# Softmax applied after the value product: a change of staging in a fused cross-attention and FP4 feed-forward kernel

## The chip, the cores and the metric

The kernel runs on one core of a Trainium2 chip. The metric is the device time of one execution in microseconds, the median of several runs. TensorE is called PE below, VectorE DVE in the rows, ScalarE ACT, GpSimd POOL and SyncE SP.

## The reference

`x` is (2, 1024, 256), the context (2, 154, 256), with 16 heads of 64 columns.

```python
def xattn(query, key, value, ...):
    q = einsum("bnd,hdk->bhnk", query, proj_q) + bias_q      # k, v from the context in the same way
    logits = einsum("bhqk,bhnk->bhqn", q, k) / sqrt(64)
    heads = einsum("bhqn,bhnv->bhqv", softmax(logits), v)    # 154 keys
    return concat(heads) @ w_out.T
x = x + xattn(layernorm(x), ctx, ctx, ...)
x = x + ffn(layernorm(x), w_gate, w_up, w_down)              # FP4 block quantisation, silu(gate) * up, width 704
```

## The kernel before

**Precision.** Every matrix product but the transposes is made of three f16 products. A tile in f32 is split into a high half (a cast to f16, mostly by ScalarE) and a low half (f32 minus the high half, mostly by VectorE); `three` (L454) multiplies high by high, high by low and low by high.

**Stages.** A start (to some 31 us) loads and splits the weights, makes keys and the first queries. Then comes the loop over 64 *slots*: a slot n is one step i = n // 8 (of 8), one of two token tiles s = n // 4 % 2 of 128 rows, and one group of four heads, j = n % 4. In a step the batch is i // 4. After the loop follow 16 tiles of the FFN. Every engine has its own program, an order written out by hand, with semaphores between them.

**One slot.** PE computes the scores of four heads, 128 tokens by 4 x 154 keys (`score`, L591). VectorE takes the row maxima (`row_max`, L1036), ScalarE the exponentials with their row sums (`exps`, L805, the sums through `accum_out`), VectorE the reciprocals (`inverse`, L1042). POOL multiplies the exponentials by them (`norm`, L1297 and L1298) into `normal`, 5 chunks of 128 columns: one per head for the first 128 keys and a fifth in which the last 26 keys of the four heads lie 32 apart. The high half of `normal` is cast by ScalarE in odd slots (L816), by VectorE in even ones (L1049); the low half is made by VectorE where n % 8 is 2, 5 or 6 (L1055), by POOL in the other five of eight (L1304). SP issues one DMA transpose of both halves, 128 x 1280 f16 (`turn_p`, L435), into `pT`, keys as rows.

**Tasks.** Besides scores and projection, PE has *tasks*, each with one PSUM bank: `x` (transpose of normalised rows, L566), `q` (queries of two pairs of heads, L577, 12 matmuls of 256 columns), `v` (values, L508 to L527), `wo` (transposes of w_out, L501), `w` (FFN weights, L602, L607) and `h` (heads, L540 and L543: values as the stationary tile of 64 columns, `pT` as the moving one of 256 tokens, two heads side by side in the array, 12 such pairs; the result is heads transposed, as the projection needs it). `tasks_of(n)` lists those of a slot. The three banks 4, 5 and 7 are taken in turn (`task_bank`), and `next_task` (L492) makes PE wait until VectorE has made the low half of the task that had the bank before. ScalarE makes the high half of each task (`high`, behind its exponentials), VectorE the low half (`low`, behind the row maximum of the next slot):

```python
# PE                                   # VectorE, slot(n)
for n in range(SLOTS):                 row_max(n)                      # waits for score(n)
    score(n)                           if n >= 1: inverse(n - 1)
    if parts_of(n): project(*parts_of(n))   ...
    for t in tasks_of(n):              for t in tasks_of(n - 1): low(t)
        task(t)
```

A step before has 4 `q`, 4 `h` and 1 `x` task in its 8 slots, and in the first slots also 6 `v` (slots 0 to 5) and 4 `wo` (slots 6 to 9).

**Projection.** `project(i, p)` (L554 to L556), 6 matmuls of 256 columns per slot, adds into bank 6; `add_attention` (L1060) adds the sum to x and takes its statistics. In the slots run also, on VectorE, POOL and ScalarE, six pieces of the FFN weights' quantisation (block scales L1069 to L1073 in slot 1 of steps 1 to 6, L1131 and L1134 in slots 5 and 6, L1311, L1335, L855) and LayerNorm steps (slots 52 to 56).

Of the kernel before, what the change touches and what calls it, by code (L numbers as in the profile page):

```python
# [31 lines left out]
REST = L - P  # L32
RESTP = 32
SLOTS = 2 * STEPS * QUADS
CHUNK = 5 * P
# [64 lines left out]
def xattn_ffn_kernel(nc, x, ctx_in, proj_q, bias_q, proj_k, bias_k, proj_v, bias_v, w_out,  # L100
                     w_gate, w_up, w_down, out):
    with ExitStack() as ctx:
# [12 lines left out]
        v_h = sb("v_h", [P, B, H * DK], F16)  # L115
        v_l = sb("v_l", [P, B, H * DK], F16)
        vl_h = sb("vl_h", [P, B, QUADS, 4, DK], F16)
        vl_l = sb("vl_l", [P, B, QUADS, 4, DK], F16)
        pT = sb("pT", [P, 2, QUADS, 2, 5, 2 * P], F16)
# [10 lines left out]
        xnT_h = sb("xnT_h", [P, KC, B * P], F16)  # L130
        xnT_l = sb("xnT_l", [P, KC, B * P], F16)
        negmax = sb("negmax", [P, 2, H], F32)
        rsum = sb("rsum", [P, 2, H], F32)
        rinv = sb("rinv", [P, 2, H], F32)
# [7 lines left out]
        A2 = KC * W1 + 4 * D + F + FC * D + 2 * FP_ + 2 * FP_ + 2 * D  # L142
# [4 lines left out]
        def halves(part, n):  # L147
# [5 lines left out]
        cT_h, cT_l = (v.rearrange("p (c n) -> p c n", c=KC) for v in halves(a2[:, CT0:CT0 + KC * B * L], KC * B * L))  # L153
        ROWS0 = CT0 + KC * B * L
        ctx_rows = a2[0:L // 2, ROWS0:ROWS0 + 2 * B * D].rearrange("p (j d) -> p j d", j=2 * B)
        assert ROWS0 + 2 * B * D <= A2
        bv = pT[0:1, 1].rearrange("p j a c n -> p (j a c n)")[:, 0:4 * H * DK].bitcast(F32)
        bv_raw = bv[:, 0:H * DK]
        bv_h, bv_l = halves(bv[:, H * DK:2 * H * DK], H * DK)
        q_h, q_l = (raw["q"].bitcast(F16)[:, j * RAW:(j + 1) * RAW]  # L160
                    .rearrange("p (a t) -> p a t", a=PAIRS) for j in range(2))
        prob = arena[:, RAW:RAW + SC].rearrange("p (j n) -> p j n", j=QUADS)
        NORM0 = RAW + SC
        normal = arena[:, NORM0:NORM0 + QUADS * CHUNK].rearrange("p (j n) -> p j n", j=QUADS)
        XN0 = 4 * RAW - 4 * D
        assert NORM0 + QUADS * CHUNK <= XN0
# [3 lines left out]
        assert A2 - QUADS * CHUNK >= CT0 + KC * B * L  # L170
        hidT_h, hidT_l = (v.rearrange("p (a n) -> p a n", a=PAIRS) for v in halves(arena[:, 4 * RAW:5 * RAW], RAW))
# [23 lines left out]
        mark = [RAW]  # L195

        def over(n):
            mark[0] += n
            assert mark[0] <= XN0
            return arena[:, mark[0] - n:mark[0]]  # L200
# [29 lines left out]
        exp_done, rinv_ready, normed = sem("exp_done"), sem("rinv_ready"), sem("normed")  # L230
        high_act, high_dve = sem("high_act"), sem("high_dve")
        low_dve, low_pool = sem("low_dve"), sem("low_pool")
        turned = [sem("turned%d" % j) for j in range(QUADS)]
        proj_mm, proj_done = sem("proj_mm"), sem("proj_done")
        bv_scaled, bv_high, bv_low, ld_bv = sem("bv_scaled"), sem("bv_high"), sem("bv_low"), sem("ld_bv")
# [33 lines left out]
        def query_at(i, j):  # L269

            return 8 * (i - 1) + ((5, 6, 7, 8) if i == 1 else (4, 6, 8, 9))[j]

        def heads_at(i, j):

            return 8 * (i + 1) + (2, 3, 5, 7)[j]
# [5 lines left out]
        def tasks_of(n):  # L281

            out = [("x", i) for i in range(1, STEPS) if rows_at(i) == n]
            if n < len(VALUES): out.append(VALUES[n])
            elif n < len(VALUES) + len(WOUT): out.append(WOUT[n - len(VALUES)])
            out += [("h", i, j) for i in range(STEPS - 1) for j in range(QUADS) if heads_at(i, j) == n]
            out += [("q", i, j) for i in range(1, STEPS) for j in range(QUADS) if query_at(i, j) == n]
            out += [("w", k) for k in range(W1_JOBS) if wt_at(k) == n]
            return out

# [632 lines left out]
        def _(dve):  # L923
# [212 lines left out]
            def slot(n):  # L1136
# [3 lines left out]
                if n >= 1: inverse(n - 1)  # L1140
# [251 lines left out]
```

## Time and profile before

| | us |
|---|---|
| median of 3 runs | 429.55 (426.49 to 430.19) |
| the profiled execution | 429.8 |
| its span, first to last instruction | 427.9 |
| mean granted PE clock | 0.932 of 2.4 GHz |

The rows further down are of this one profiled execution. Times are microseconds from the start of its span; a duration marked mean is in ns. "Idle before" is time in which the engine sat idle ahead of an instruction, and the arrow names what ended it. Instructions on one engine overlap a little at their ends, so two of 0.47 us take 0.84.

### The profile page before, as it was taken

The page shows a single profiled execution, that of the slowest core. Times are in us where ns is not written, and L with a number is a line of the kernel's source. Part 1 is how long each engine was busy: PE and PEld are TensorE (multiplying, and loading weights), DVE is VectorE, ACT ScalarE, POOL GpSimd, SP SyncE. Part 2 cuts the span into 40 slices and gives each one's busy share as a digit, 9 for nine tenths or more (in the row PEclk, how much of TensorE's full clock was granted, in tenths as well). Part 3 has the DMA queues.
Part 4 walks back from the last instruction along what each step waited for, and adds up shares of the span by engine and source line. Part 5 has one row for each costly group of instructions (what it writes and reads, how often), then busy time and mean ns, then how long its engine had stood idle before and what let it go on. Part 6 is the DMA issues. An engine that isn't in the chain of part 4 may idle for free.

```text
span 427.9 us, 9077 instructions
## 1 busy us (share of the span) xinstructions
PE 337.4 (79%) x3371; PEld 250.3 (58%) x3371; DVE 363.5 (85%) x652; ACT 259.6 (61%) x821; POOL 273.2 (64%) x275
## 2 busy tenths in 40 slices
PE   1865877876969969869687698198877999999985
PEld 1542355665747757757465466076655766677764
DVE  2989558899999997999999969448999999999692
ACT  4756578877787877877884678334351545543331
POOL 3453455897888878978886568613592767686710
PEclk9999589998998979999999669689998999999999
DMA  7970343455554464655543434600000000000001
GB/s 218 323 282 1 63 92 63 82 105 96 93 102 86 93 117 86 109 84 91 106 85 73 93 63 92 123 2 2 2 0 15 12 26 12 21 19 12 27 25 38
DMA packets 92413, 32.44 MB, mean 76 GB/s; under 512 B 84492, under 2 KB 90320, under 8 KB 92369
## 3 DMA queue, kind: packets, MB, share of 16 engines
q1 hardware_dynamic: 92369, 31.86, 34.7%
q8 instruction: 27, 0.44, 0.4%
q14 instruction: 17, 0.14, 0.1%
HBM read 8.78 MB, written 2.10 MB: 25 GB/s over the span
## 4 chain that ended last, share of the span: by engine, by line
DVE 58%; PE 18%; POOL 14%; issue 5%; ACT 3%; DMA 1%; SPq 0%; DVEq 0%; POOLq 0%
DVE negmax L1036 6%; POOL arena L1304 5%; POOL arena L1298 5%; DVE arena L1049 5%; DVE arena L1055 4%; DVE arena L1112 4%; DVE arena L1114 4%; DVE arena L998 3%; PE ps L456 3%; PE ps L458 3%; PE ps L591 3%; PE ps L457 3%; DVE arena L1027 3%; DVE arena L1238 3%; DVE blk_h L1069 2%
## 5 line engine op out<-in xcount | busy, mean ns | idle before, releaser
L805 ACT ACTIVATE arena<-ps,negmax 128x154 f32<-128x154 f32 x256 | 96.5, 395 | 46.8 <-DVE negmax L1036 46.5
L1297 POOL TENSOR_TENSOR arena<-arena,rinv 128x104 f32<-128x104 f32 x64 | 30.1, 470 | 64.5 <-DVE rinv L1042 64.5
L1298 POOL TENSOR_TENSOR arena<-arena,rinv 128x512 f32<-128x512 f32 x64 | 70.5, 1102 | 0.0
L1036 DVE TENSOR_REDUCE negmax<-ps 128x4 f32<-128x616 f32 x64 | 50.2, 785 | 20.5 <-PE ps L591 20.3
L1304 POOL TENSOR_TENSOR arena<-arena 128x640 f16<-128x640 f32 x40 | 63.7, 1592 | 0.8 <-ACT arena L816 0.8
L591 PE MATMUL ps<-kT_h,arena 64*128 64x154 f16 x512 | 39.8, 241 | 28.6 <-DVE arena L1027 18.7
L805 ACT ACTIVATION_READ_ACCUMULATOR arena<-ps,negmax 128x1 f32 x256 | 53.8, 210 | 0.0
L591 PEld LDWEIGHTS ps<-kT_h,arena 64*128 64x128 f16 x512 | 24.0, 98 | 44.9 <-DVE arena L1027 27.0
L456 PE MATMUL ps<-arena,xnT_h 128*128 128x352 f16 x128 | 40.1, 313 | 3.2 <-DVE xnT_l L1122 3.2
L456 PE MATMUL ps<-xnT_h,wq_h 128*128 128x256 f16 x128 | 36.2, 283 | 7.9 <-DVE wot_l L984 2.5
L456 PE MATMUL ps<-arena 128*128 128x256 f16 (+2 forms) x120 | 36.1, 301 | 7.8 <-DVE arena L937 5.9
L457 PE MATMUL ps<-arena,xnT_h 128*128 128x352 f16 x128 | 40.0, 313 | 0.0
L458 PE MATMUL ps<-arena,xnT_l 128*128 128x352 f16 x128 | 40.0, 312 | 0.0
L540 PE MATMUL ps<-pT,v_h 128*64 128x256 f16 x256 | 35.7, 288 | 3.8 <-DVE wot_l L984 1.6
L554 PE MATMUL ps<-wot_h,arena 128*128 128x256 f16 x128 | 37.8, 295 | 1.0 <-DVE arena L998 0.3
L555 PE MATMUL ps<-wot_l,arena 128*128 128x256 f16 x128 | 37.5, 293 | 0.0
L556 PE MATMUL ps<-wot_h,arena 128*128 128x256 f16 x128 | 37.4, 292 | 0.0
L876 ACT ACTIVATE arena<-ps 128x704 f32<-128x704 f32 x16 | 12.1, 756 | 41.4 <-PE ps L458 41.4
L457 PE MATMUL ps<-xnT_l,wq_h 128*128 128x256 f16 x128 | 36.3, 283 | 0.0
L458 PE MATMUL ps<-xnT_h,wq_l 128*128 128x256 f16 x128 | 36.2, 283 | 0.0
L457 PE MATMUL ps<-arena 128*128 128x256 f16 (+2 forms) x120 | 36.0, 300 | 0.0
L458 PE MATMUL ps<-arena 128*128 128x256 f16 (+2 forms) x120 | 35.9, 299 | 0.0
(155 smaller groups left out, 1030.5 us busy)
## 6 DMA issues: line engine op xcount, KB each, us to landing
out_dram<-arena SPq DMA_DIRECT2D x16, 128.0 KB, 1.7
xs<-in_x_dram SPq DMA_DIRECT2D x2, 512.0 KB, 7.2
arena<-in_L_xattn_w_out_dram SPq DMA_DIRECT2D x1, 1024.0 KB, 11.8
pT<-arena SPq DMA_TRANSPOSE x64, 3.4
xs<-in_x_dram SPq DMA_DIRECT2D x2, 384.0 KB, 6.6
wffn<-in_L_ffn_w_down_dram SPq DMA_DIRECT2D x1, 704.0 KB, 9.5
wffn<-in_L_ffn_w_gate_dram SPq DMA_DIRECT2D x1, 640.0 KB, 7.8
wffn<-in_L_ffn_w_up_dram SPq DMA_DIRECT2D x1, 640.0 KB, 8.4
```

Source lines behind the costliest of these rows:

```text
L456: pe.matmul(o, a_h, b_h, start=start, stop=False)
L457: pe.matmul(o, a_h, b_l, start=False, stop=False)
L458: return pe.matmul(o, a_l, b_h, start=False, stop=stop)
L540: pe.matmul(o[u * DK:(u + 1) * DK, k * 256:(k + 1) * 256], vh[:, b, h * DK:(h + 1) * DK], pT[:, i % 2, j, part, 2 * k + u], start=n == 0, ...
L554: pe.matmul(o, a_h, wot_h[:, p], start=p == 0 and s == 0, stop=False, skip_group_check=True)
L555: pe.matmul(o, a_h, wot_l[:, p], start=False, stop=False, skip_group_check=True)
L556: last = pe.matmul(o, a_l, wot_h[:, p], start=False, stop=p == PAIRS - 1, skip_group_check=True)
L591: last = pe.matmul(ps[:, 2 * (j % 2) + u, k * L:(k + 1) * L], q[r, p, s * P:(s + 1) * P], kt[r, batch(i), p], start=n == 0, stop=n == 2)
L805: last = act.activation(prob[:, j, k * L:(k + 1) * L], ps[:, 2 * (j % 2) + k % 2, (k // 2) * L:(k // 2 + 1) * L], ACT.Exp, bias=negmax[:, ...
L1036: dve.tensor_reduce(negmax[:, s, 4 * j:4 * j + 4].rearrange("p (k u) -> p u k", k=2), v, AX.X, ALU.max, negate=True).then_inc(max_done, 1)
L1298: pool.tensor_tensor(main_of(normal, j), v[:, :, 0:P], r.to_broadcast([P, 4, P]), ALU.mult).then_inc(normed, 1)
L1304: pool.tensor_tensor(part_of(j, 1), normal[:, j], part_of(j, 0), ALU.subtract).then_inc(low_pool, 1)
```

## The change

- ScalarE's exponentials no longer give row sums and go unnormalised into `prob`, where the four heads now lie 160 columns apart: 640 columns, 5 full chunks of 128. They are split right there: the high half by ScalarE in every slot, the low half by VectorE where n % 4 is 1, else by POOL. POOL's `norm` is gone.
- The values are laid out to fit these chunks, in 8 parts, each with 64 columns, a column of ones and one of padding (`HB` = 66), zero where a chunk's row belongs to another head. Heads are one task per slot: `pT` is the stationary tile (128 keys by 128 tokens), the values are the moving one, of 66 or 132 columns, 5 chunks times 3 products. Tokens are now the rows of the result, and the ones give the row sum in column 64 of each head.
- VectorE takes the reciprocal of the sums and multiplies heads by it, 128x256 from PSUM to SBUF (`scale_hid`). ScalarE casts the high half, POOL subtracts the low half, and SP transposes both by DMA (128 x 512 f16, `turn_hid`); the projection reads the result.
- Heads of slot n are computed in slot n + 5, projected in slot n + 10 (after the slot's tasks rather than ahead of them). Queries of steps 2 to 7 are tasks of one pair, one per slot; their buffers, and those of the turned rows, are doubled. Values of batch 0 are tasks of slots 0 to 3, of batch 1 of slots 11 to 14 (each 16 matmuls of 256 columns); w_out is turned in slots 6, 8, 9 and 10.
- `task_bank` and `next_task` stay as they are.

```diff
+LP = 160
+CHUNK = 4 * LP
+CHUNKS = CHUNK // P
+RING_P = 2 * QUADS
+HB = DK + 2
+HEADS_LAG = 5
+PROJ_LAG = 10
+PARTS = [(c, a) for c in range(CHUNKS) for a in range(4) if c * P < (a + 1) * LP and (c + 1) * P > a * LP]
...
-        VALUES = [("v", b, n) for b in range(B) for n in range(3)]
+        VALUES = [("v", b, n) for b in range(B) for n in range(4)]
+        def values_at(b, n):
+            return n if b == 0 else 11 + n
+        def wot_at(n):
+            return (6, 8, 9, 10)[n]
         def rows_at(i):
-            return 8 * (i - 1) + (3 if i == 1 else 2)
+            return 3 if i == 1 else 8 * (i - 1) - 1
+        def query_at(i, p):
+            return 4 + p // 2 if i == 1 else 8 * (i - 1) + 1 + p
+        def pairs_of(i):
+            return 2 if i <= 1 else 1
...
+            out += [t for t in VALUES if values_at(t[1], t[2]) == n]
+            out += [t for t in WOUT if wot_at(t[1]) == n]
+            out += [t for i in range(1, STEPS) for t in query_tasks(i) if query_at(i, t[2]) == n]
+            out += [("h", n - HEADS_LAG)] if HEADS_LAG <= n else []
...
         def low_by_dve(n):
-            return n % 8 in (2, 5, 6)
+            return n % 4 == 1
...
+            def turn_hid(n):
+                i, s, j = place(n)
+                sp.wait_ge(hid_low, n + 1)
+                if n >= RING_P: sp.wait_ge(proj_mm, n - RING_P + 1)
+                sp.dma_start_transpose(hidT[:, j, :, :, s * P:(s + 1) * P].rearrange("p a k n -> p (a k) n"),
+                                       hsplit[:, j]).then_inc(hid_turned[j], 16)
             for n in range(SLOTS):
-                turn_p(n)
+                if n >= 1: turn_p(n - 1)
+                if n >= HEADS_LAG + 2: turn_hid(n - HEADS_LAG - 2)
...
+            def heads(n):
+                i, s, j = place(n)
+                b = batch(i)
+                pe.wait_ge(turned[j], 16 * (n // QUADS + 1))
...
+                o = next_task(("h", n))
+                order = range(CHUNKS)
+                parts = ((v_h, 0), (v_l, 0), (v_h, 1))
+                for k, (v, part) in enumerate(parts):
+                    for c in order:
+                        at = [m for m, (chunk, a) in enumerate(PARTS) if chunk == c]
+                        h0, h1 = PARTS[at[0]][1], PARTS[at[-1]][1] + 1
+                        last = pe.matmul(o[:, h0 * HB:h1 * HB], pT[:, s, j, part, c],
+                                         v[:, b, j, at[0]:at[-1] + 1].rearrange("p m k -> p (m k)"),
+                                         start=k == 0 and c == order[0], stop=k == 2 and c == order[-1], skip_group_check=True)
+                last.then_inc(task_mm, 1)
...
             for n in range(SLOTS):
                 score(n)
-                if parts_of(n): project(*parts_of(n))
                 for t in tasks_of(n):
                     task(t)
+                if n >= PROJ_LAG: project(n - PROJ_LAG)
...
                 i, m = divmod(n, 8)
-                if n >= 2 and high_by_act(n - 2): high_p(n - 2)
+                if n >= 1: high_p(n - 1)
+                if n >= HEADS_LAG + 2: high_hid(n - HEADS_LAG - 2)
                 exps(n)
...
+            def inverse(n):
+                dve.wait_ge(task_mm, TASK_AT[("h", n)] + 1)
+                dve.reciprocal(rinv[:, n % 2].unsqueeze(2), per_head(n)[:, :, DK:DK + 1]).then_inc(rinv_ready, 1)
+            def scale_hid(n):
+                dve.wait_ge(rinv_ready, n + 1)
+                wait(dve, hid_low, n - 1)
+                dve.tensor_tensor(hidden_f[:, n % 2].rearrange("p (r k) -> p r k", r=4), per_head(n)[:, :, 0:DK],
+                                  rinv[:, n % 2].unsqueeze(2).to_broadcast([P, 4, DK]), ALU.mult).then_inc(task_low, 1)
...
                 row_max(n)
-                if n >= 1: inverse(n - 1)
-                if n >= 2 and not high_by_act(n - 2): high_p(n - 2)
+                if n >= HEADS_LAG + 1: inverse(n - HEADS_LAG - 1)
                 if n >= 1:
                     for t in tasks_of(n - 1):
                         low(t)
-                if n >= 2 and low_by_dve(n - 2): low_p(n - 2)
+                if n >= 1 and low_by_dve(n - 1): low_p(n - 1)
...
-                if n >= 1: norm(n - 1)
-                if n >= 2 and not low_by_dve(n - 2): low_p(n - 2)
+                if n >= 1 and not low_by_dve(n - 1): low_p(n - 1)
+                if n >= HEADS_LAG + 2: low_hid(n - HEADS_LAG - 2)
```

Of the last slots' heads, those of slots 59 to 63 are tasks of the FFN's first three tiles (2, 2 and 1), and the projections of slots 56 to 63 follow there in pairs, in the first four tiles; each waits for its DMA transpose.

## Rows read from the trace of the kernel before

**Rows 1.** page, part 1: busy us (share of the span), instructions, by engine
```profile
PE 337.4 (79%) x3371; PEld 250.3 (58%) x3371; DVE 363.5 (85%) x652; ACT 259.6 (61%) x821; POOL 273.2 (64%) x275
```

**Rows 2.** windows, one loop step: PE, PEld, DVE, ACT, POOL busy; clock, DMA share, GB/s
```profile
165.70:193.40 27.70, 23.05 (x306) 18.39 (x304) 26.78 (x49) 22.11 (x85) 22.83 (x25) 1.00 0.58 96
```

**Rows 3.** costliest groups, 60 to 305 us: xcount | busy us, mean ns | idle before
```profile
L1298 POOL TENSOR_TENSOR arena<-arena,rinv 128x512 f32<-128x512 f32 x58 | 64.3, 1109 | 0.0
L1304 POOL TENSOR_TENSOR arena<-arena 128x640 f16<-128x640 f32 x37 | 59.5, 1607 | 0.8 <-ACT arena L816 0.8
L805 ACT ACTIVATION_READ_ACCUMULATOR arena<-ps,negmax 128x1 f32 x229 | 48.3, 211 | 0.0
...
L1049 DVE CAST arena<-arena 128x640 f16<-128x640 f32 x29 | 28.4, 979 | 1.8 <-POOL arena L1298 1.1
L1297 POOL TENSOR_TENSOR arena<-arena,rinv 128x104 f32<-128x104 f32 x58 | 27.5, 473 | 47.0 <-DVE rinv L1042 47.0
L1055 DVE TENSOR_TENSOR arena<-arena 128x640 f16<-128x640 f32 x23 | 26.8, 1165 | 0.0
...
L1027 DVE SCALAR_TENSOR_TENSOR arena<-ps,biasT,arena 128x256 f16<-128x256 f32 x56 | 23.8, 466 | 0.0
...
L816 ACT ACTIVATE arena<-arena 128x640 f16<-128x640 f32 x30 | 22.6, 754 | 4.6 <-POOL arena L1298 4.6
L998 DVE TENSOR_TENSOR arena<-ps,arena 128x512 f16<-128x512 f32 x32 | 21.7, 680 | 0.1
...
L765 ACT ACTIVATE arena<-ps 128x512 f16<-128x512 f32 x32 | 19.6, 616 | 4.6 <-PE ps L543 4.6
```

**Rows 4.** chain of waits, 57 to 70 us: start us, us, what
```profile
63.58 0.80 DVE negmax L1036
...
64.47 0.59 DVE wot_l L984
65.05 0.14 issue
65.19 0.27 PE ps L456
65.46 0.11 PE ps L457
...
66.66 0.53 PE ps L591 x12
```

**Rows 5.** timeline, VectorE, row maximum of slots 8, 16, 33, 34, 48, 63
```profile
67.21 0.80 DVE L1036 TENSOR_REDUCE negmax<-ps 128x4 f32<-128x616 f32 x1 [0.62 <-PE ps L591]
...
94.48 0.78 DVE L1036 TENSOR_REDUCE negmax<-ps 128x4 f32<-128x616 f32 x1
...
154.39 0.79 DVE L1036 TENSOR_REDUCE negmax<-ps 128x4 f32<-128x616 f32 x1
...
158.47 0.73 DVE L1036 TENSOR_REDUCE negmax<-ps 128x4 f32<-128x616 f32 x1
...
205.64 0.78 DVE L1036 TENSOR_REDUCE negmax<-ps 128x4 f32<-128x616 f32 x1
...
265.16 0.78 DVE L1036 TENSOR_REDUCE negmax<-ps 128x4 f32<-128x616 f32 x1
```

**Rows 6.** the transposes' line: duration ns of the issue; us to landing
```profile
L435 SPq DMA_TRANSPOSE pT<-arena x64: 1320/1339/2344, 43.1 to 274.6; - x64
...
DMA to landing us min/median/max: 3.3/3.4/5.1
```

**Rows 7.** timeline, PE, 137 to 152 us: two pairs of score matmuls
```profile
138.41 0.24 PE L591 MATMUL ps<-kT_h,arena 64*128 64x154 f16 x2
138.49 0.23 PE L591 MATMUL ps<-kT_l,arena 64*128 64x154 f16 x2
```

**Rows 8.** timeline, POOL, start: its first subtraction and the idle time before it
```profile
12.63 2.11 POOL L1283 TENSOR_TENSOR pT<-pT 1x1024 f16<-1x1024 f32 x1 [8.15 <-ACT pT L732]
```

**Rows 9.** timeline, PE, 264 to 303 us: first transpose of the FFN
```profile
275.69 0.69 PE L641 MATMUL ps<-ident,arena 128*128 128x128 f32 x2 [8.81 <-POOL arena L1319]
```

More of the change, by code:

```diff
@@ new lines, in fourth @@
+                def fourth(part, a):
+                    return part.rearrange("p (j r k) -> p r j k", r=4, k=DK)[:, a]
+                for u, (chunk, a) in enumerate(parts_of_values(n)):
+                    out_u = o[:, u * 256:(u + 1) * 256].rearrange("p (j k) -> p j k", k=DK)
+                    keys = slice(chunk * P % LP, chunk * P % LP + P)
+                    for c in range(KC):
+                        three(out_u, cT_h[:, c, b, keys], cT_l[:, c, b, keys], fourth(wv_h[:, c], a), fourth(wv_l[:, c], a),
+                              c == 0, False)
+                    pe.matmul(out_u, ones[:, :], fourth(bv_h, a), start=False, stop=False)
+                    last = pe.matmul(out_u, ones[:, :], fourth(bv_l, a), start=False, stop=True)
@@ L547, in project @@
[L547 to L553 removed]
+                pe.wait_ge(turned[j], 16 * (n // QUADS + 1))
+                if i % (STEPS // B) == 0 and s == 0 and j == 0:
+                    pe.wait_ge(task_low, TASK_AT[("v", b, 3)] + 1)
@@ new lines, in heads, with project @@
+                last.then_inc(task_mm, 1)
+            def project(n):
+                i, s, j = place(n)
+                pe.wait_ge(hid_turned[j], 16 * (n // QUADS + 1))
+                if n < QUADS: pe.wait_ge(task_low, TASK_AT[("wo", n)] + 1)
+                if s == 0 and j == 0: wait(pe, proj_done, i)
+                o = ps[:, PROJ_BANK, s * D:(s + 1) * D]
+                for k in range(2):
+                    p = 2 * j + k
+                    a_h, a_l = (hidT[:, j, part, k, s * P:(s + 1) * P] for part in range(2))
@@ L583, in score @@
                 if s == 0:
-                    pe.wait_ge(task_low, TASK_AT[("q", i, j)] + 1)
+                    pe.wait_ge(task_low, TASK_AT[("q", i, 2 * j + 2 - pairs_of(i))] + 1)
                 wait(pe, exp_done, m - 1)
+                q_h, q_l = (queries(i)[:, part] for part in range(2))
                 for k in range(2):
@@ L613, in task @@
                 if t[0] == "q": query(t[1], t[2])
[L614 removed]
+                if t[0] == "h": heads(t[1])
                 if t[0] == "w": turn_weights(t[1])
@@ L621, in task @@
                         pe.wait_ge(ones_ready, 1)
-                    values(t[1], t[2]) if t[2] < 2 else rest_values(t[1])
+                        pe.wait_ge(ctx_wide, 1)
+                    values(t[1], t[2])
             turn_x(0)
             pe.wait_ge(w_low, 2)
-            for j in range(QUADS):
-                query(0, j)
+            for t in query_tasks(0):
+                query(0, t[2])
             pe.wait_ge(job_low, J_END)
@@ L700, in _ @@
             turn_xq(0, 1)
-            for p in range(4, PAIRS):
-                project(STEPS - 2, p)
+            for n in range(PROJ_BODY, PROJ_TAIL[0][0]):
+                project(n)
             steps(pe, ffn, first=3)
@@ L849, in slot @@
                     high(t)
-                if m == (2 if i == 0 else 0) and exists(i + 1):
-                    if i == 0: act.wait_ge(ln_step, 2 * LN_STEPS)
-                    normalised(xn, i + 1, xn_ready)
+                if n == 2: act.wait_ge(ln_step, 2 * LN_STEPS)
+                for r in range(1, STEPS):
+                    if rows_at(r) - (1 if r == 1 else 2) == n: normalised(xn, r, xn_ready)
                 if m == 4 and 0 < i <= W_STEPS:
```

363 lines of the change are left out of this document (169 added, 194 removed).

## The prediction, made before the changed kernel was run

> **What bounds the kernel now.** I first read the share of the span by engine [rows 1]: VectorE is the busiest at 85%, no other engine is above 79%. Then the windows: of the 27.70 us of one loop step (8 slots), VectorE works 26.78, PE 23.05, ScalarE 22.11, POOL 22.83 [rows 2]. So the loop is VectorE's, nearly without gaps: casts and subtractions [rows 3] and the row maximum, 0.8 us per slot [rows 4]. The reader should see next that a second limit already shows: the chain of waits from 63.58 us on. Row maximum of slot 7, reciprocal, low half of a task (L984), 12 matmuls of the next task, which waited for the PSUM bank that this low half freed, 12 score matmuls, row maximum of slot 8 at 67.21 [rows 4, 5]. That ring took 3.63 us and holds no work of VectorE beyond 1.5 us. Tasks take three banks in turn, so a task waits for the low half of the task three before it. Now that is nearly always two or more slots back (9 tasks in 8 slots), so the ring is rare.
>
> **The change, part by part.**
> *POOL.* Out go both multiplications, 0.47 + 1.11 us per slot, 12.6 us per step. In come one more low half in eight (40 become 48 in all; 1.61 us) and a 128x256 subtraction per slot, 256/640 of 1.61 = 0.64 us, 5.2 us per step [rows 3]. 22.8 becomes about 17 us.
> *ScalarE.* Out go the 32 reads of the accumulator per step. They overlap their neighbours; the gain lies between 0.09 and 0.21 us each, and I take 0.09: 2.9 us. Out go 4 casts of heads, 2.5 us. In come 4 casts of 128x640 (0.75 us, 3.0) and 8 of 128x256 (between 0.3, which is 256/640 of that, and 0.75; part of it is fixed, so I take 0.35: 2.8) [rows 3]. Net 0: 22 us.
> *VectorE.* Out per step: 4 casts (0.98 us with their waits, 3.9), one of three low halves (1.17), 4 subtractions of 128x512 (0.60 each beyond the overlap, 2.4). In: 8 multiplications of 128x256 from PSUM, between 0.38 (L1027, 0.47 less 0.09 of overlap) and 0.60 (L998); they are like L1027, 0.38, so 3.0 us [rows 3]. 26.8 becomes about 22.3 us.
> *DMA.* One transpose more per slot, 4 blocks of 128 columns beside 10. SP took 1.34 us to issue one of ten; both make 1.9 us, an estimate by blocks. The DMA share of 0.58 is 2.0 us per slot [rows 2, 6]; with 14 blocks for 10 it is 2.8 us. Both lie under 3.4 us. A landing took 3.3 to 5.1 us [rows 6] and may take more, but heads come 5 slots after the exponentials and the projection 5 slots after the heads: some 18 us each, cover enough. Without that cover, it would be the DMA rival below.
> *PE, columns.* Heads were 12 pairs of 256 columns for two slots, 0.66 us per slot. Now they are 15 matmuls of 66 or 132 columns per slot, 1584 columns. Floor: 0.11 us per 256 columns [rows 4], so 0.68 us. Ceiling: no 128-row matmul with another stationary tile comes closer than 0.11 us in the rows, 1.64 us. Between them stand the score pairs of 154 columns, 0.07 us apart [rows 7]. They are nearest in width: 1.0 us. The Trainium skill, "TensorE: Matmul & The Clock Gate", section Back-to-back issue gap, gives about 81 ns per 128-column matmul where each loads its weights; by that, heads would cost 1.2 us and the total 10 us more. The trace of before has no such f16 matmul.
> *PE, order.* This decides. Queries of steps 2 to 7 are now one pair per task, so each slot has two tasks, a query and then heads (a third with x, w_out or values). Three banks remain. Walking down the list: heads of slot n take the bank of the query of slot n-1, in nearly every slot from 17 to 56. VectorE gives that bank free only after row maximum n, and this waits for score n, which stands before the heads on PE. So the rare ring closes in every slot, and behind the blocked heads stand the projection (6 x 0.11 = 0.66 us) and score n+1.
>
> **The ring, priced.** From the 3.63 us of [rows 4, 5]: the low half L984 (0.59) becomes one of a query (0.38), -0.21; 12 matmuls (1.31) become 1.0 + 0.66, +0.35; one more change of task on PE, +0.1 (66.66 less 65.19 less 1.31 leaves 0.16). That is 3.87 us per slot. VectorE's own work in a plain slot is 0.71 + 0.08 + 0.38 + 0.38 = 1.6 us, and 3 to 3.8 us with a low half or a step of the weights: all under the ring. Only the slot with the block scales stays as it was, 154.39 to 158.47, 4.08 us [rows 5], as two low halves of queries become one and one multiplication. Slot 7 of each step also has its query behind the previous one's low half: +0.65, 4.52. Slot 0 has its query behind the low half of x (0.6 for 0.38) and then heads behind that: 4.74. A step is 5 x 3.87 + 4.08 + 4.52 + 4.74 = 32.7 us, against (205.64 - 94.48)/4 = 27.8 now [rows 5].
>
> **The sum**, against the profiled execution, 429.8 us:
> - Slots 0 to 7: nearly as now, values of batch 1 leave, heads and a longer wait come: +1.5 (-5 to +5). POOL first has more to do, larger memsets, nine small ones and two copies of the context; it sat idle 8.15 us before its first subtraction [rows 8], which hides them (at worst some 2 us are left over).
> - Slots 8 to 15: here three tasks ask for three banks, so each waits for its own kind of the slot before. A value task is 16 x 0.11 = 1.75 us, inside the ring with the query's 0.65 and 0.4 more for its low halves: 6.7 us. Four value slots 26.6, w_out slots 4.1, 4.3 (no projection yet) and 5.4 (a w_out task taken as long as a query), the last, with x, 5.8: 46.2 against 94.48 - 67.21 = 27.3. +18.9.
> - Slots 16 to 47: 4 x 4.9 = +19.6.
> - Slots 48 to 63: the first four as above, +1.9; then LayerNorm steps on VectorE bound both kernels, and without its casts it does them sooner, -2.6. -0.7.
> - After the last slot: from row maximum 63 to the first transpose of the FFN lay 10.5 us [rows 5, 9], POOL's chain of two normalisations and a low half. It becomes maximum, exponentials, two casts, one low half and the rounding, 5.1 us. The FFN's first tiles now carry heads that go through ScalarE, POOL and a DMA before they are projected: -5 (0 to -10).
> Sum +34.3: **464 us**, also against the median of 429.55, which the profiled time equals. PE's share of the ring is 2.4 us. The clock in the window of [rows 2] was full; each tenth of the slots at 1.2 GHz would add some 12 us, each tenth now hidden. I put none into the sum and keep it in the range.
>
> **Rivals.**
> 1. *The banks come free in time, VectorE stays the bound* (11%). For it: it loses 4.5 us per step and everything else has room. Then 26.8 - 4.5 + 0.9 of gaps = 23.2 us per step, 4.6 x 6 + 5 = 33 us less, 397 us. Against it: the order of waits, written out in the kernel. It decides if the low half of a query falls ahead of the next row maximum.
> 2. *PE's small matmuls at 0.11 us* (6%): +0.64 in some 52 slots, 497 us. For it: every 128x128 tile is loaded anew and the load's record is 0.10 us. Against: score pairs load two such tiles per 0.07.
> 3. *The DMA queue becomes the bound* (2%): if transposes don't overlap, 3.4 + 2 us per slot, over 520 us. Against: the share above.
> 4. *The ring bites less and other gains even it out* (5%): within 1%, 430 us. It needs a floor price in all slots and no loss in slots 8 to 15.
> That the change doesn't do what it says I exclude: the counts follow from the code.
>
> **How the numbers follow.** The forecast has 76%. Its low end: heads at the floor, -0.32 in 45 slots, slots 0 to 7 at -5 rather than +1.5, the end at -7: 440. Its high end: half of the way to rival 2, or a tenth to two tenths at half clock: 488. That leaves out rival 1 and little else. A measurement of this kernel tells about 1% from no change. Faster 0.11, same 0.05, slower 0.84.
>
> **What would show it.** Right: steps of 32 to 33 us between the row maxima of slots 16 and 48; in the waits, PE at the heads' line for VectorE's low half of the query, in nearly each slot, 0.5 us or more each, 30 us in all; VectorE busy under 75%, idle before the row maximum for the score; slots 8 to 15 over 42 us; heads' matmuls 0.06 to 0.08 us apart. Wrong: steps under 27 us, no wait at the heads' line, VectorE busy over 85%; or the longest waits behind a landing.

## The result, and the profile after

The changed kernel takes 465.22 us (median of 4 runs, 464.86 to 468.54) against 429.72 (4 runs, 426.49 to 430.19): ratio 1.086, 95% interval 1.079 to 1.093. The forecast was 464, slower. The profiled execution is the slowest of the four, 468.54 us with a span of 466.7; a second profile of the same kernel (the last experiment) has a span of 461.2, and the difference is told below.

The page of the changed kernel: busy time by engine, the clock granted to TensorE in 40 slices, and the chain that ended last, by engine.
```profile
PE 356.7 (76%) x3595; PEld 263.9 (57%) x3595; DVE 319.5 (68%) x650; ACT 264.2 (57%) x635; POOL 227.8 (49%) x232
...
PEclk9989599876899999999999899987988899999999
...
PE 49%; DVE 36%; issue 8%; ACT 3%; DMA 1%; POOL 1%; SPq 0%; DVEq 0%; ACTq 0%
```
VectorE fell from 85% to 68% [rows 1], and no engine took its place as the bound: each works a smaller share of a longer span. Half the chain is now PE. One loop step of the new kernel (PE, PEld, DVE, ACT, POOL busy; clock, DMA share, GB/s):
```profile
159.30:190.40 31.10, 23.13 (x317) 17.81 (x318) 19.85 (x43) 22.42 (x60) 17.07 (x18) 1.00 0.68 118
```
Against [rows 2], VectorE lost 6.9 us of work in a step (19.85 for 26.78; 22.3 was foreseen, and the difference is explained at the end), POOL 5.8 (17.07 for 22.83), PE and ScalarE are as before, and the step is 3.4 us longer. So work left and time came: look at waits. The row maxima of the slots of [rows 5], slots 8, 16, 33, 34, 48 and 63, in the timeline of VectorE:
```profile
70.62 0.80 DVE L1078 TENSOR_REDUCE negmax<-ps 128x4 f32<-128x616 f32 x1 [2.56 <-PE ps L626]
...
123.85 0.80 DVE L1078 TENSOR_REDUCE negmax<-ps 128x4 f32<-128x616 f32 x1 [4.13 <-PE ps L626]
...
190.41 0.80 DVE L1078 TENSOR_REDUCE negmax<-ps 128x4 f32<-128x616 f32 x1 [2.17 <-PE ps L626]
193.91 0.80 DVE L1078 TENSOR_REDUCE negmax<-ps 128x4 f32<-128x616 f32 x1 [0.44 <-PE ps L626]
...
248.25 0.80 DVE L1078 TENSOR_REDUCE negmax<-ps 128x4 f32<-128x616 f32 x1 [2.56 <-PE ps L626]
...
306.46 0.80 DVE L1078 TENSOR_REDUCE negmax<-ps 128x4 f32<-128x616 f32 x1 [1.08 <-PE ps L626]
```
The idle time before them, released by the score's matmuls (L626), is the new thing. The waits of the whole execution (engine, line, what it waited for: us in total, times, longest) put 105.8 us on it:
```profile
DVE negmax L1078 <- PE ps L626: 105.8, 58, 6.4
...
PE ps L572 <- DVE q_odd L1070: 14.5, 19, 2.4
...
PE ps L572 <- DVE arena L1070: 8.9, 13, 0.7
PE ps L587 <- DVE xs L1106: 8.7, 6, 1.6
...
PE ps L493 <- DVE v_l L1037: 5.5, 3, 2.2
```
L1070 is the low half of a query, L572 the heads. PE stands there 32 times, 23.4 us in all: 24 times in the 32 slots from 16 to 47, 0.7 us at a time, and up to 2.4 us in the others. One plain slot in the timeline shows the whole ring:
```profile
171.39 0.80 DVE L1078 TENSOR_REDUCE negmax<-ps 128x4 f32<-128x616 f32 x1 [1.91 <-PE ps L626]
...
172.11 0.17 DVE L1088 RECIPROCAL rinv<-ps 128x4 f32<-128x4 f32 x1
172.20 0.45 DVE L1070 SCALAR_TENSOR_TENSOR arena<-ps,biasT,arena 128x256 f16<-128x256 f32 x1
...
172.80 0.40 PE L572 MATMUL ps<-v_h,pT 128*128 128x66 f16 x5 [0.69 <-DVE arena L1070]
...
173.53 0.27 PE L587 MATMUL ps<-wot_h,arena 128*128 128x256 f16 x1
...
174.27 0.24 PE L626 MATMUL ps<-kT_h,q_odd 64*128 64x154 f16 x2
...
174.89 0.80 DVE L1078 TENSOR_REDUCE negmax<-ps 128x4 f32<-128x616 f32 x1 [1.91 <-PE ps L626]
```
Row maximum at 171.39, reciprocal, low half of the query; that frees the bank, 15 heads matmuls in 0.73 us (172.80 to 173.53), projection 0.74, score, and the next row maximum at 174.89: 3.50 us, of which VectorE works 1.6.

By parts, in us (first line: up to row maximum 8):

| part | before | forecast | first profile | second profile |
|---|---|---|---|---|
| slots 0 to 7 and all ahead of them | 67.2 | 68.7 | 70.6 | 68.3 |
| slots 8 to 15 | 27.3 | 46.2 | 53.2 | 50.2 |
| slots 16 to 47 | 111.2 | 130.8 | 124.4 | 125.2 |
| slots 48 to 63 | 59.5 | 58.8 | 58.2 | 59.3 |
| after row maximum 63 | 162.7 | 157.7 | 160.2 | 158.2 |
| span | 427.9 | 462.2 | 466.7 | 461.2 |

### The profile page after: what moved, and what is told of

It reads as the page before. It is cut to its first block, busy times and chain, and to the rows that moved or that the text cites. A ratio compares the mean times of both kernels' runs of the same rounds, so it can differ in the third digit from the quotient of the medians.

```text
span 466.7 us, 9583 instructions
## 1 busy us (share of the span) xinstructions
PE 356.7 (76%) x3595; PEld 263.9 (57%) x3595; DVE 319.5 (68%) x650; ACT 264.2 (57%) x635; POOL 227.8 (49%) x232
## 4 chain that ended last, share of the span: by engine, by line
PE 49%; DVE 36%; issue 8%; ACT 3%; DMA 1%; POOL 1%; SPq 0%; DVEq 0%; ACTq 0%
PE ps L572 9%; PE ps L493 8%; PE ps L626 7%; PE ps L495 7%; PE ps L494 6%; DVE arena L1161 4%; DVE arena L1163 3%; PE ps L587 3%; PE ps L588 3%; PE ps L589 3%; DVE arena L1283 2%; DVE arena L1249 2%; DVE q_odd L1070 2%; DVE rinv L1088 2%; DVE arena L1101 2%
## 5 line engine op out<-in xcount | busy, mean ns | idle before, releaser
L1078 DVE TENSOR_REDUCE negmax<-ps 128x4 f32<-128x616 f32 x64 | 51.1, 799 | 105.9 <-PE ps L626 105.8
L840 ACT ACTIVATE arena<-ps,negmax 128x154 f32<-128x154 f32 x256 | 78.6, 391 | 67.4 <-DVE negmax L1078 67.1
L572 PE MATMUL ps<-v_h,pT 128*128 128x132 f16 (+1 forms) x640 | 53.4, 215 | 28.1 <-DVE q_odd L1070 14.5
L1360 POOL TENSOR_TENSOR arena<-arena 128x256 f16<-128x256 f32 x64 | 45.9, 720 | 38.9 <-ACT arena L857 38.9
L572 PEld LDWEIGHTS ps<-v_h,pT 128*128 128x128 f16 x640 | 38.9, 100 | 38.5 <-issue 37.1
L493 PE MATMUL ps<-arena 128*128 128x256 f16 (+1 forms) x144 | 42.8, 297 | 14.6 <-DVE arena L983 6.1
L850 ACT ACTIVATE arena<-arena 128x640 f16<-128x640 f32 x64 | 47.9, 749 | 0.1
L493 PE MATMUL ps<-arena,xnT_even 128*128 128x352 f16 x128 | 41.1, 321 | 4.2 <-DVE xnT_even L1171 4.2
L587 PE MATMUL ps<-wot_h,arena 128*128 128x256 f16 x128 | 36.9, 288 | 8.7 <-DVE xs L1106 8.7
L494 PE MATMUL ps<-arena 128*128 128x256 f16 (+1 forms) x144 | 42.8, 297 | 0.0
L495 PE MATMUL ps<-arena 128*128 128x256 f16 (+1 forms) x144 | 42.8, 297 | 0.0
L494 PE MATMUL ps<-arena,xnT_even 128*128 128x352 f16 x128 | 40.9, 320 | 0.0
L495 PE MATMUL ps<-arena,xnT_even 128*128 128x352 f16 x128 | 40.8, 319 | 0.0
L857 ACT ACTIVATE arena<-arena 128x256 f16<-128x256 f32 x64 | 27.1, 427 | 5.5 <-DVE arena L1094 5.5
L1367 POOL TENSOR_TENSOR arena<-arena,blk_h 128x704 f32<-128x704 f32 x15 | 28.5, 1902 | 1.2
L1411 POOL TENSOR_TENSOR arena<-arena,blk_h 128x704 f32<-128x704 f32 x15 | 23.4, 1561 | 10.3 <-DVE arena L1163 10.3
L493 PE MATMUL ps<-xnT_even,wq_h 128*128 128x256 f16 x64 | 19.1, 299 | 10.4 <-DVE xnT_odd L1138 5.0
```

What stands on the lines that cost most here:

```text
L493: pe.matmul(o, a_h, b_h, start=start, stop=False)
L494: pe.matmul(o, a_h, b_l, start=False, stop=False)
L495: return pe.matmul(o, a_l, b_h, start=False, stop=stop)
L572: last = pe.matmul(o[:, h0 * HB:h1 * HB], pT[:, s, j, part, c], v[:, b, j, at[0]:at[-1] + 1].rearrange("p m k -> p (m k)"), start=k == 0 a ...
L587: pe.matmul(o, a_h, wot_h[:, p], start=p == 0 and s == 0, stop=False, skip_group_check=True)
L840: last = act.activation(prob[:, j, k * LP:k * LP + L], ps[:, 2 * (j % 2) + k % 2, (k // 2) * L:(k // 2 + 1) * L], ACT.Exp, bias=negmax[:, ...
```

## The experiments

Theory: the ring. The heads of slot n wait for a PSUM bank that VectorE frees only after row maximum n, and score n+1 stands behind them. Rivals: VectorE's own work still sets the slot; only the order on PE counts, not the bank; small matmuls cost more than taken. All runs are whole kernels; the kernel before took 430.4 to 431.5 us (medians) beside them. Experiments 1 to 9 and 12 are one execution each, so differences of a few us between their totals say little; the steps, which repeat within a profile, say more. Where one profile is compared, step means the distance of row maxima eight slots apart, between slots 16 and 48.

**1. The score one slot ahead.**
```diff
+            score(0)
             for n in range(SLOTS):
-                score(n)
+                if n + 1 < SLOTS: score(n + 1)
                 for t in tasks_of(n):
                     task(t)
```


> Edit: TensorE issues the score of slot n+1 before the tasks of slot n, so that it no longer stands behind heads that wait for their bank; the heads keep their wait, and no arithmetic changes. Ring theory: the row maximum of slot n+1 no longer depends on the low half made after the row maximum of slot n. A step of slots 16 to 47 falls from 31.1 us to what the busiest engines need (PE 23.1, ACT 22.4 in that stretch), with some joints left: 24 to 27 us, so 16 to 28 us off these four steps; slots 8 to 15 lose 10 us or more of their 53.2; whole kernel 425 to 440 us. Rival, VectorE's own work or a DMA sets the slot: the step stays at 30 to 31 us and the kernel within 5 us of 465.

Measured: 398.4 us, step 23.3 (24.4 in the fourth, with slots 40 to 47). One step, and slots 8 to 15 (columns as above):
```profile
59.87:92.00 32.13, 30.23 (x375) 22.89 (x374) 24.30 (x53) 27.50 (x76) 17.55 (x17) 1.00 0.75 118
...
115.31:138.56 23.25, 22.19 (x317) 18.16 (x316) 19.96 (x44) 21.93 (x61) 17.59 (x18) 1.00 0.95 147
```
and its waits from slot 16 to 47:
```profile
DVE rinv L1089 <- PE ps L572: 9.3, 17, 0.7
...
PE ps L587 <- DMA arena<-arena: 3.2, 4, 1.4
...
DVE negmax L1079 <- PE ps L626: 0.9, 4, 0.2
```
VectorE waits 0.9 us in all for scores there, in 32 slots, instead of 1.9 us in each plain slot. The heads still ask for the same banks, in the same order; only what stood behind them is gone. The ring theory holds, and its expectation was too small: the step came out under its 24 to 27 us, and I had counted the steps from 16 to 47 (now 94.3 us for 124.4) and something of slots 8 to 15 (32.1 for 53.2), and forgotten that slots 0 to 7 (59.9 for 70.6 with all ahead of them) and 48 to 63 (48.7 for 58.2) hold the same ring.

**2. The heads twice.**
```diff
-                parts = ((v_h, 0), (v_l, 0), (v_h, 1))
+                parts = ((v_h, 0), (v_l, 0), (v_h, 1), (v_h, 0), (v_l, 0), (v_h, 1))
```


> Edit: the 15 matmuls of a slot's heads are issued twice into the same accumulation (30), numerator and sum of exponentials both doubled, so that their quotient is unchanged. It measures what heads cost where they stand. Ring theory: the heads lie between the wait for the bank and the next score, so their 0.73 us is paid in full in each slot of slots 8 to 57: a step of slots 16 to 47 rises from 31.1 to 36 to 37 us (8 x 0.73 = 5.8), the kernel by 30 to 45 us, to 495 to 510. Rival, another engine sets the slot and TensorE has room: under 10 us in all.

Measured: 491.6 us, 3.4 us under the expected range. A plain slot went from 3.50 to 4.23 us, exactly the 0.73 that 15 matmuls take. The step rose by 4.45, not 5.8, for the third slot became shorter (4.43 for 5.07). There the added matmuls lie beside another wait, which the next experiment names, and this wait itself fell by 0.63 us: a low half of VectorE (L1101) that took 1.45 us in the changed kernel took 0.82 here. So the heads are on the path, and 15 matmuls of 66 or 132 columns, each with a 128x128 tile of its own, cost 0.049 us each. The kernel rose by 26 us.

**3. All low halves by GpSimd.**
```diff
         def low_by_dve(n):
-            return n % 4 == 1
+            return False
```


> Edit: the low half that VectorE makes in one slot of four goes back to GpSimd, so VectorE has 1.1 us less in every fourth slot, and GpSimd makes all 64. Ring theory: VectorE makes that low half after the query's, and waits for the next score afterwards; so nothing changes, step 30.5 to 31.5 us and the kernel within 3 us of 465. Rival, VectorE is still what bounds: 1.1 us off in each of 16 slots, 12 to 18 us faster. Rival, GpSimd's low half sets the arrival of the turned exponentials: slower by more than 5 us.

Measured: 447.1 us, a miss: 16 to 18 us faster, where I expected nothing. The size is that of the first rival, but the place is not. Of the two slots of a step in which VectorE makes a low half, the seventh stayed at 3.50 us; the third fell from 5.07 to 3.70. The chain through the third slot of the changed kernel (start, us, what):
```profile
163.71 0.37 DVE arena L1070
...
164.41 1.37 DVE arena L1101
165.78 0.61 DVE xs L1106
...
166.53 0.27 PE ps L587
...
167.34 0.51 PE ps L626 x12
```
and through a third slot here (slot 18):
```profile
123.14 0.38 DVE q_odd L1070
...
123.66 0.89 PE ps L572 x15
...
124.59 0.27 PE ps L587
```
L1101 is VectorE's low half, L1106 the addition of the step's attention, L587 the first projection of the next step, which waits for that addition because both use one bank, and the next score stands behind it. The low half, 1.37 us, is in the path only where the addition is queued behind it. That is a second ring of the same kind.

The two slots differ in one thing more. The low half takes 1.45 us in the third slot, in each of the four steps, and 0.81 or 0.82 in the seventh. What runs beside it in the third is GpSimd's multiplication of a weight tile (L1367). First the changed kernel, then experiment 2, where the longer slots let L1367 all but end before the low half begins:
```profile
163.71 1.39 POOL L1367 TENSOR_TENSOR arena<-wffn,blk_w 128x704 f32<-128x704 f32 x1
...
164.33 1.45 DVE L1101 TENSOR_TENSOR arena<-arena 128x640 f16<-128x640 f32 x1
```
```profile
170.61 1.38 POOL L1367 TENSOR_TENSOR arena<-wffn,blk_w 128x704 f32<-128x704 f32 x1
...
171.95 0.82 DVE L1101 TENSOR_TENSOR arena<-arena 128x640 f16<-128x640 f32 x1
```
So some 0.63 of the 1.37 us is VectorE's instruction taking longer while GpSimd's runs. By parts, experiment 3 against the second profile of the changed kernel: slots 16 to 47 -6.3 us, slots 48 to 63 -5.7, slots 8 to 15 -6.2; the last is partly something else, and comes under experiment 12.

**4. The addition first.**
```diff
                 row_max(n)
+                if m == (PROJ_LAG + 8) % 8 and n >= PROJ_LAG + 8: add_attention((n - PROJ_LAG - 8) // 8)
                 if n >= HEADS_LAG + 1: inverse(n - HEADS_LAG - 1)
...
-                if m == (PROJ_LAG + 8) % 8 and n >= PROJ_LAG + 8: add_attention((n - PROJ_LAG - 8) // 8)
```


> Edit: VectorE adds the attention of a step directly after the row maximum of the third slot of the step, ahead of its reciprocal and low halves. The first projection of each step waits for it, and the next score stands behind that projection. Theory of a missed wait: the third slot falls from 5.07 us by 0.5 to 1.2 us (the projection's wait of 1.5 us goes, the low halves come later by the 0.7 us of the addition, in part on the ring), 3 to 7 us off the kernel. Rival, the long third slot comes of the weights' scales made by VectorE in the second slot: no change beyond 1 us.

Measured: 462.0 us. The third slot is 4.88 for 5.07, 0.2 us a step, where 0.5 to 1.2 were expected. The projection no longer waits for the addition at all, but the addition, with the row statistics in the same function, now stands ahead of the query's low half, that is in the first ring: PE waits 31.0 us at the heads' line for that low half, where it was 23.4. The wait moved from one ring into the other; the theory named the right wait and priced the way out wrongly.

**5. Queries two pairs to a task.**
```diff
-            return 4 + p // 2 if i == 1 else 8 * (i - 1) + 1 + p
+            return 4 + p // 2 if i == 1 else 8 * (i - 1) + 2 + p
...
-            return 2 if i <= 1 else 1
+            return 2
```


> Edit: the queries are again made two pairs to a task, in every second slot (as in the kernel before), instead of one pair in every slot; TensorE's order is otherwise that of the changed kernel, and the same matmuls are issued. With 13 tasks in a step instead of 17, of the heads of slots 16 to 47 only two in eight find that their bank was last used in the slot before, against eight in eight. Ring theory: step of slots 16 to 47 from 31.1 to 24 to 27 us, kernel 430 to 445 us. Rival, what matters is the work that stands ahead of a score (the same here) and not the bank: step 30 to 32 us, kernel within 5 us of 465.

Measured: 451.5 us, step 29.6 to 30.1: between the two expectations, and not settled by itself. The heads' waits for queries fell from 23.4 to 8.5 us, as the theory says, and the idle time before row maxima from 105.8 to 83.3. But the third slot grew to 5.2 to 6.0 us; its chain:
```profile
151.81 1.60 DVE arena L1101
153.40 0.61 DVE xs L1106
...
154.15 0.27 PE ps L587
```
VectorE comes to the low half sooner, while more of GpSimd's L1367 (151.34 to 152.73) is still to run, and the instruction takes 1.68 us (1.60 in the path) for 0.81 in the seventh slot; the projection waits for the addition 2.9 us at worst. The granted clock, too, is 0.90 in these steps, where the changed kernel had 1.00. Thus part of the gain went to the second ring and part to the clock; how much to each, this run can't say.

**6. Score ahead, all low halves by GpSimd; 7. score ahead, addition first; 8. score ahead, queries in pairs.** The edits are those of 1 with 3, 4 and 5.

> Edit: score of slot n+1 ahead of the tasks of slot n, and all 64 low halves by GpSimd. In the run with the score ahead alone a step is 23.3 us, with PE 22.2, ACT 21.8, DVE 20.0, POOL 17.7 busy. Theory: there VectorE's low half of 1.1 us waits in the seventh slot (5.0 us) for ScalarE's high half and holds the next row maximum; without it the step falls to 22.3 to 22.8, and the kernel by 3 to 8 us, to 390 to 396. Rival, TensorE and ScalarE hold the step already: within 2 us of 398. Rival, GpSimd's 1.4 us per slot become the bound: 400 to 410.

> Edit: score of slot n+1 ahead of the tasks of slot n, and VectorE's addition of a step's attention directly after the row maximum of the third slot. With the score ahead the first projection's wait for that addition holds no score any more. Theory: no change, 396 to 400 us. Rival, the projection's wait still holds the heads of the next slot and so the banks: 2 to 5 us faster.

> Edit: score of slot n+1 ahead of the tasks of slot n, and queries two pairs to a task. Ring theory: both edits break the same ring, so the second adds little on the first: 392 to 402 us against 398. Rival, they act on different waits: their gains add up, below 385 us.

Measured: 397.3, 400.4 and 407.3 us, against 398.4 for the score ahead alone. Four executions of the score ahead alone (experiment 11) spread from 397.6 to 403.0, so the first two totals can't be told from it. Run 6 missed its theory's 390 to 396 and met its first rival; run 7 ended at the upper edge of its 396 to 400, with steps of 23.7 to 23.8. The third experiment's 16 us are gone once the score is ahead: both rings cost only through the score behind them. In run 6 the first two steps are faster, 22.0 and 22.5 us, and the later ones slower, 24.6 and 25.5. Two windows of run 6 (columns as above):
```profile
92.00:115.00 23.00, 22.91 (x334) 19.01 (x333) 18.66 (x44) 22.33 (x62) 19.31 (x20) 1.00 1.03 148
138.00:163.00 25.00, 22.20 (x318) 18.23 (x316) 19.38 (x43) 23.35 (x66) 21.00 (x21) 1.00 0.89 154
```
PE works 22.9 of the first 23 us, so TensorE is at its limit there. The DMA share is 1.03 beside it; whether that is a limit too no run shows. In the second stretch neither is full; what slows it I have not traced. Run 8 fell outside its expectation, 5 us above it: query tasks of double length leave uneven slots (1.25 to 5.40 us), step 25.1.

**9. Heads first, the score where it was.** The heads become the first task of a slot, and VectorE makes their reciprocal and product ahead of the row maximum.
```diff
-                row_max(n)
-                if n >= HEADS_LAG + 1: inverse(n - HEADS_LAG - 1)
+                if n >= HEADS_LAG + 1:
+                    inverse(n - HEADS_LAG - 1)
+                    low(("h", n - HEADS_LAG - 1))
+                row_max(n)
                 if n >= 1:
                     for t in tasks_of(n - 1):
-                        low(t)
+                        if t[0] != "h": low(t)
```
(in tasks_of the line of "h" stands ahead of all others)

> Edit: in each slot the heads are the first task instead of the last, and VectorE makes their reciprocal and product before the row maximum of the next slot; the score stays where it is in the changed kernel. From slot 17 the heads find a bank last used two slots back, and the query one that the heads of the slot before used, which VectorE has cleared before the row maximum. Ring theory: the same gain without touching the score: step of slots 16 to 47 from 31.1 to 25 to 27.5 us (two of eight slots, beside the task x, keep a ring), slots 8 to 15 keep theirs through the values: 44 us at full clock, up to 53 if the clock falls again; kernel 435 to 452 us. Rival, the ring was the score's place in TensorE's order and any task in front of it costs the same: step 30 us or more.

Measured: 426.5 us, step 26.8 as expected; the kernel below the expected 435 to 452, in part since slots 8 to 15 took 38.6 and the clock did not fall in them, and since slots 48 to 63, which the expectation left out, took 50.6. One step:
```profile
133.15:159.95 26.80, 22.60 (x319) 18.22 (x319) 20.68 (x43) 22.33 (x61) 17.53 (x17) 1.00 0.85 135
```
Here PE's order still has the score behind every task. What changed is which low half frees the bank and how early VectorE makes it, and that was enough for 4.3 us a step. It leaves no room for the rival that only the order on PE counts, which wanted 30 us or more. Experiments 1 and 9 break the ring at two different places, and both free the step.

**10. Heads first and score ahead; 11. the score ahead alone, timed.**

> Edit: heads first (with their product before the row maximum) and the score of slot n+1 ahead of the tasks of slot n. With the score ahead TensorE is busy 22.2 us of a step of 23.3 already. Theory: TensorE is then the bound, nothing more than 0 to 1 us a step: 390 to 400 us. Rival, waits of TensorE for the banks still cost in slots 8 to 15 (32 us there): below 388 us. Rival, the reciprocal ahead of the row maximum makes VectorE wait for heads that TensorE makes later: 400 to 410 us.

> Edit: only the score of slot n+1 ahead of the tasks of slot n, timed in rounds. Expected: 396 to 401 us, ratio to the kernel before 0.92 to 0.935.

Measured: 412.6 us, ratio 0.958 (0.956 to 0.960), and 399.2 us, ratio 0.929 (0.923 to 0.935), each from 4 runs against 7 of the kernel before. Together they are worse than the score ahead alone, by somewhat more than the second rival gave, and for another reason. The waits of run 10:
```profile
DVE arena L1095 <- POOL arena L1363: 27.6, 30, 1.9
```
The product of the heads (L1095) waits for GpSimd's low half of the product two slots before, 30 times; set ahead of the row maximum, this wait holds it. (In experiment 11, where the product stands behind the row maximum, it waits 2.2 us in all.) So none of the versions made is shown to be faster than the one with one edit, the score of the next slot ahead of the tasks: 7% below the kernel before.

**12. The changed kernel again.**

> Edit: none; the changed kernel, profiled a second time. In its first profile slots 8 to 15 took 53.2 us, with a granted TensorE clock of 0.79, 0.66, 0.65 and 0.74 in slots 11, 13, 14 and 15; with all low halves by GpSimd they took 44.0 us at clock 1.00; with the addition moved 50.2 us, slot 14 at full clock. Theory: the order of the work fixes what the slots take at full clock, and the clock's fall adds to it, not the same each time: slots 16 to 47 again 31.1 us a step to within 0.1, slots 8 to 15 between 44 and 54 us and as long as their clock says. Rival, the fall belongs to the program: the same four slots at the same clock, 53.2 us to within 0.5.

Measured: 463.0 us, span 461.2; steps 31.1, 31.1, 31.9 and 31.1. Slots 11 to 15 of the first profile (PE, PEld, DVE, ACT, POOL busy; clock, DMA share, GB/s):
```profile
82.93:90.90 7.97, 6.40 (x55) 4.38 (x55) 2.19 (x6) 3.29 (x9) 2.69 (x4) 0.79 0.62 109
90.90:97.41 6.51, 4.88 (x55) 3.43 (x55) 2.25 (x7) 3.84 (x10) 0.63 (x2) 1.00 0.38 73
97.41:107.54 10.13, 7.97 (x55) 4.91 (x55) 3.64 (x9) 4.97 (x13) 2.52 (x3) 0.66 0.24 45
107.54:117.24 9.70, 7.96 (x55) 5.05 (x55) 3.97 (x9) 3.39 (x9) 2.37 (x4) 0.65 0.25 50
117.24:123.85 6.61, 4.79 (x43) 3.78 (x43) 2.44 (x6) 3.23 (x8) 3.40 (x4) 0.74 0.36 69
```
slots 11, 13 and 14 of the second:
```profile
80.56:88.53 7.97, 6.41 (x55) 4.28 (x55) 2.19 (x5) 3.29 (x9) 2.54 (x3) 0.79 0.64 109
...
95.04:105.17 10.13, 7.97 (x55) 4.92 (x55) 3.65 (x9) 4.97 (x13) 2.37 (x3) 0.66 0.23 45
105.17:111.78 6.61, 4.88 (x55) 3.42 (x55) 3.96 (x9) 3.39 (x9) 1.01 (x2) 1.00 0.39 71
```
and of the run with all low halves by GpSimd:
```profile
82.69:89.14 6.45, 4.88 (x55) 3.42 (x55) 2.19 (x5) 3.29 (x9) 2.02 (x3) 1.00 0.55 73
...
95.65:102.69 7.04, 4.88 (x55) 3.42 (x55) 3.65 (x9) 4.45 (x12) 2.02 (x2) 1.00 0.33 65
102.69:109.30 6.61, 4.88 (x55) 3.42 (x55) 3.23 (x7) 3.90 (x11) 2.71 (x3) 1.00 0.37 73
109.30:114.39 5.09, 3.26 (x43) 2.77 (x43) 2.44 (x7) 3.23 (x8) 3.39 (x4) 1.00 0.47 90
```
Slots 11 and 13 are equal to 0.01 us in both profiles (and in experiment 4), at a clock of 0.79 and 0.66; slot 14 is 9.70 us at 0.65 or 6.61 at 1.00. At full clock (third fence) the slots take 6.45, 7.04, 6.61 and 5.09. Neither theory holds alone: the fall in slots 11, 13 and 15 came in all three profiles of this order on PE (the third is experiment 4's), that in slot 14 in one of them. One step in slots 16 to 47 also took 31.9 where "within 0.1" was expected. The row maximum of slot 0 also moved back, from 33.90 to 31.68, where the kernel before has 31.67: the clock of that stretch was 0.95 in the first profile and 1.00 in the second. Experiments 2, 3, 5 and 8 have the late start at 0.95 too, the others not.

## Why the prediction was right, point by point

- *The bound.* Right: the ring that was rare closes in every slot, and the chain of [rows 4] is its picture. VectorE busy 68% (forecast: under 75%), idle before the row maximum for the score, steps of 31.1 us (32 to 33). Experiment 1 shows the cause from the other side: with the score out of the ring the step is 23.3 us and the kernel 398 to 399. Rival 1 gave 23.2 and 397 for the case that banks come free in time. That its numbers meet this kernel is luck: they stood on VectorE as the bound with 22.3 us of work in a step, and in experiment 1 VectorE works 20.0 us of 23.25, ScalarE 21.9 and PE 22.2. Of the signs named, three came short: steps of 31.1 us for 32 to 33, 23.4 us of waits at the heads' line for 30, matmuls 0.049 us apart for 0.06 to 0.08.
- *The plain slot, 3.87.* It measured 3.50. The term that was mis-sized most is the heads: taken as 1.0 us, they measured 0.73, nearly the column floor of 0.68, not near the score pairs of [rows 7]. The changes from task to task on PE, 0.26 in the sum (0.16 and 0.1), measured 0.08 between 172.80 and 174.27; smaller terms were a little too cheap. The Trainium skill, "TensorE: Matmul & The Clock Gate", section Back-to-back issue gap, gives about 81 ns for a matmul of 128 columns that loads its own weights; by that, 15 would take 1.2 us, an estimate from the page. The trace disagrees, with 0.049 us a matmul of 66 or 132 columns (106 on average). Seven of the eight slots of a step, the three loaded ones too, came 0.36 to 0.58 us under the forecast.
- *VectorE's work, 22.3 us a step.* It measured 19.85, and three instructions on weight tiles make most of the difference: block scales 0.19 us (L1117) for 1.25 (L1071), and 0.94 and 0.88 (L1180, L1183) for 1.50 and 1.44 (L1131, L1134). The sum took them as unchanged, but in the kernel before each ran with GpSimd's L1298 or L1304 beside it from end to end. So "only the slot with the block scales stays as it was, 4.08" failed: that slot is 3.50 us like the plain ones, on the ring.
- *The third slot of a step.* Missed: forecast 3.87, measured 5.07. The sentence that put VectorE's slots "with a low half" all under the ring overlooked that the low half stands ahead of the addition, and the projection waits for that; and the low half takes 1.45 us there, beside GpSimd's L1367. Experiment 3 removes 1.37 us there. The two errors, -2.8 and +1.2 us a step, partly cancel: 31.1 for 32.7.
- *Slots 8 to 15, +18.9.* The mechanism and its sizes were right at full clock: 44.0 us in experiment 3 against 46.2; value slots 6.5 to 7.0 (6.7 forecast), slots 8 to 10 3.8, 3.7 and 4.8 (4.1, 4.3, 5.4), slot 15 5.1 (5.8). What was put at nothing and left to the range was the clock: it fell in slots 11, 13 and 15, and in the first profile in 14. The same four slots are 9.2 us longer there than in experiment 3 (1.5 + 3.1 + 3.1 + 1.5), 6.2 in the second profile.
- *Slots 0 to 7, +1.5.* Second profile +1.0. The first profile's +3.4 holds 2.2 of the late start at clock 0.95, which the same kernel did not have in the second.
- *Slots 48 to 63, -0.7.* Measured -1.3 and -0.2, within what two profiles differ.
- *The end, -5.* The first transpose of the FFN comes 6.0 us after row maximum 63 (5.1 forecast, 10.5 before [rows 5, 9]):
```profile
312.50 0.69 PE L677 MATMUL ps<-ident,arena 128*128 128x128 f32 x2 [3.00 <-POOL arena L1375]
```
  Over the whole end -4.5 in the second profile, -2.5 in the first. I have not traced the 2 us between them.
- *Small matmuls at 0.11 us* (rival 2): excluded by experiment 2. *The DMA queue* (rival 3): the share is 0.68 in the step, and no engine waits for a landing in slots 16 to 47; it reaches about 1.0 only in the kernels with the score ahead, where a step is 22 to 23 us; in experiment 1 the projection waits 3.2 us in all for landings in slots 16 to 47.

So the sum of 34.3 was near for partly wrong reasons: plain slots too dear by some 11 us over slots 16 to 47, the third slot and the clock too cheap by 5 and 6 to 9 us. That these cancel to within 2 us of the median is luck; the ring and its place are not.

## To carry to other kernels

Before work is taken off the busiest engine, walk the in-order queue of the engine that feeds it: list for each task which buffer it takes, who frees it, and what stands behind the task while it waits. Here a task list that grew from 9 to 16 or 17 tasks a step on three banks turned a saving of 7 us of VectorE's work a step into a loss of 3.4, and issuing the next score ahead of the tasks that may block made it 7% faster than the old kernel. An instruction whose engine has time to spare can still be in the path if another engine waits for the one queued behind it.

## What the runs showed of the hardware, unexpected

- Matmuls of 66 and 132 columns in f16, each with a stationary 128x128 tile of its own, run at 0.24 us for five, 0.049 us each, close to their columns at 0.11 us per 256: the tile loads add nothing that shows. At half clock fifteen took 1.34 us (104.33 to 105.67, slot 13 of the first profile) for 0.73.
- The granted clock fell to half of full speed (1.2 of 2.4 GHz, 256-column matmuls 0.21 us apart for 0.11) in parts of slots 11 and 13, in which PE had first waited 1.6 and 2.2 us for a bank and was then busy; but slot 12, with the same matmuls and a wait of 1.6, ran at full clock, and so did all of them in experiment 3, with the same waits to 0.01 us (1.57, 1.63, 2.15 in slots 11, 12, 13) and the same busy time of 4.88 us in 6.5 to 7.0. Slots 16 to 47, with shorter waits of 0.7 us, stayed at 1.00. What sets it off is open. Filling the waits with matmuls that do nothing would be the test; it wasn't tried, as no PSUM bank stands free in those slots.
- Where an instruction of VectorE and one of GpSimd, both on operands in SBUF, fall together, the one that began first keeps its time and the other takes longer by most of the overlap. VectorE's low half of 128x640 took 0.82 us alone, 1.45 where GpSimd's L1367 had 0.78 us still to run and 1.68 where it had 1.0. In the seventh slot of experiment 5 the two begin within 0.01 us, VectorE's low half takes its 0.81 and GpSimd's 128x256 subtraction 1.34 to 1.35 for 0.67. VectorE's product of the heads, which reads PSUM, took 0.41 us beside that subtraction at its 0.67 (172.37 to 173.04). The mean of 1.61 us for GpSimd's low half in [rows 3] mixes 1.40, as in the changed kernel, with 2.05 where VectorE's L1131 or L1134 had begun before it.
- The 16 DMA engines' share reached 1.03 with two transposes in each slot of 2.8 us, and those of the exponentials still landed in 3.5 us (median of experiment 6; 3.8 in experiment 1, 3.4 in the kernel before).
